# Second mixture of experts on one core: w2 is split one expert ahead, in pieces on ScalarE and GpSimd

## What is computed

```python
logits = flat_x @ Wg + bg
top_vals, top_idx = jax.lax.top_k(logits, TOPK)          # TOPK = 2 of E = 4
probs = jax.nn.softmax(sparse, axis=-1)                  # over the two chosen
for i in range(E):
    score = jnp.where(assigned, probs[:, i], -jnp.inf)
    sel_p, sel_idx = jax.lax.top_k(score, capacity)      # capacity = 256 tokens
    p = jnp.where(jnp.isfinite(sel_p), sel_p, 0.0)[:, None]
    tok = flat_x[sel_idx]
    h = jax.nn.gelu(tok @ W1[i], approximate=False)      # 256 -> 1024
    y = h @ W2[i] * p                                    # 1024 -> 256
    out = out.at[sel_idx].add(y)
```

## Time and profile before

| | us |
|---|---|
| median of 3 runs | 693.44 (691.79 to 694.69) |
| the profiled execution | 689.28 |
| its span, from the first to the last instruction | 687.5 |
| mean granted clock of TensorE | 0.902 |
| busy in the span: PE 589.1, DVE 518.8, ACT 358.8, POOL 183.3 | |

### The profile page before, as it was taken

The page is one execution under the profiler, slowest core; times in us unless marked ns, Lnnn a source line. Parts: engine busy times, 40 slices in busy tenths (PEclk is TensorE's granted clock), DMA queues, the critical chain, the costliest instruction groups (busy, mean ns, idle before and its releaser), DMA issues. The chain is left out here.

```text
span 687.5 us, 12671 instructions
## 1 busy us (share of the span) xinstructions
PE 589.1 (86%) x4686; PEld 403.4 (59%) x4686; DVE 518.8 (75%) x1029; ACT 358.8 (52%) x691; POOL 183.3 (27%) x296
## 2 busy tenths in 40 slices
PE   3989999996589999958989999999999857987793
PEld 2745555554467888856744444444444624976782
DVE  4788888875658766674678999999994587877636
ACT  3226777773344334342214878888888261443452
POOL 4334555562023222130500111111010000234550
PEclk9959999999589999986975999999999955998998
DMA  4534554621231211001520434424421431044331
GB/s 163 67 88 68 86 86 84 92 65 46 54 115 46 61 50 49 0 1 61 65 29 2 65 48 65 61 49 69 58 64 39 135 120 68 1 147 146 92 77 61
DMA packets 27541, 47.15 MB, mean 69 GB/s; under 512 B 13232, under 2 KB 18464, under 8 KB 26208
## 3 DMA queue, kind: packets, MB, share of 16 engines
q1 hardware_dynamic: 22112, 39.11, 27.5%
q0 software_dynamic: 4288, 7.20, 3.9%
q10 hardware_dynamic: 1088, 0.13, 0.1%
HBM read 25.22 MB, written 7.83 MB: 48 GB/s over the span
## 5 line engine op out<-in xcount | busy, mean ns | idle before, releaser
L467 ACT ACTIVATE probs<-ps 128x512 f32<-128x512 f32 x448 | 213.3, 561 | 79.2 <-PE ps L384 78.8
L360 PE MATMUL ps<-k_stack,q_stack 62*128 62x512 f32 x448 | 174.5, 466 | 7.5 <-DVE row_max L563 3.3
L384 PE MATMUL ps<-q_stack,k_stack 64*128 64x512 f32 x448 | 160.1, 435 | 9.8 <-ACT probs L467 5.9
L563 DVE TENSOR_REDUCE row_max<-ps 128x1 f32<-128x1024 f32 x128 | 149.8, 1214 | 16.2 <-PE ps L360 16.2
L384 PEld LDWEIGHTS ps<-q_stack,k_stack 64*128 64x128 f32 x448 | 76.1, 190 | 81.9 <-ACT probs L467 65.2
L399 PE MATMUL ps<-probs,v_ones 128*32 128x256 f32 (+7 forms) x2048 | 116.4, 344 | 1.9 <-ACT probs L467 1.0
L360 PEld LDWEIGHTS ps<-k_stack,q_stack 62*128 62x128 f32 x448 | 80.0, 200 | 37.6 <-DVE row_max L563 16.5
L560 DVE CUSTOM_DVE_ANT_0 y_sums<-ps,wide_mask 128x1024 f32<-128x1024 f32 (+7 forms) x128 | 91.4, 755 | 13.1 <-PE ps L360 11.8
L399 PEld LDWEIGHTS ps<-probs,v_ones 128*32 128x32 f32 x2048 | 51.5, 110 | 44.5 <-issue 14.0
L518 POOL TENSOR_SCALAR_AFFINE_SELECT probs<-probs 128x128 f32<-128x128 f32 x128 | 39.3, 313 | 46.4 <-ACT probs L467 45.1
L899 POOL TENSOR_TENSOR w_chunk_l_m<-y_sums,w_chunk_h_m 128x512 fp32r<-128x512 f32 (+1 forms) x24 | 24.3, 1039 | 101.5 <-ACT w_chunk_h_m L957 94.3
(11 more groups left out here) (208 smaller groups left out, 1125.1 us busy)
## 6 DMA issues: line engine op xcount, KB each, us to landing
y_sums<-in_w_experts SPq DMA_DIRECT2D x8, 1024.0 KB, 5.2
y_sums<-in_w_chunks SPq DMA_DIRECT2D x12, 384.0 KB, 3.1
q_stack<-part_rows SPq DMA_DIRECT2D x32, 128.0 KB, 3.4
k_stack<-part_rows SPq DMA_DIRECT2D x32, 128.0 KB, 3.9
head_sums<-sums POOLq DMA_DIRECT2D x28, 128.0 KB, 2.0
q_stack<-part_rows SPq DMA_DIRECT2D x32, 64.0 KB, 4.0
k_stack<-part_rows SPq DMA_DIRECT2D x32, 64.0 KB, 3.9
q_stack<-max_rows SPq DMA_DIRECT2D x128, 2.0 KB
```

The source lines that it names most:

```text
L360: mm = pe.matmul(scores_bank(s, a, b), stack("q_stack", h, slice(0, TOP))[:, qt * P:(qt + 1) * P], stack("k_stack", h, slice(0, TOP))[:, a ...
L384: pe.matmul(bank(at % 3, 0, b - a), stack("k_stack", h, slice(0, SIDE))[:, kt * P:(kt + 1) * P], stack("q_stack", h, slice(0, SIDE))[:, a: ...
L467: act.activation(probs[:, t % 4, a:b], bank(at % 3, 0, b - a), ACT.Exp).then_inc(exp_done, 1)
L563: dve.tensor_reduce(row_max[:, h % 2, qt:qt + 1], scores_bank(s, 0, end), AX.X, ALU.max).then_inc(scores_free, 1)
```

## The change

Four edits, all in `mixture_1`:

- **w2 one expert ahead.** ACT makes w2's high part of expert e + 1 in four pieces (`split_piece`), one behind each quarter's GELU copy of expert e; the single instruction behind `split_slots` is gone. POOL makes the low quarter of expert e + 1 behind `g_l` of the same quarter of expert e (expert 0's behind `row_ready`, before the experts begin).
- **POOL's order.** `fetch(e + 1)` stands one quarter earlier in POOL's queue, and `add_rows(e - 1)` ahead of expert e's quarters, as before.
- **SP's order.** For experts 2 and 3, w2 is loaded in front of w1.
- **Unread products.** Seven go in front of TensorE's wait for the probabilities, three between `row(0)` and `ranks(0)`, and those in `ranks(0)` go from 14 to 7, with none behind the last three tiles.

```diff
--- before.py
+++ after.py
@@ -1139,7 +1139,7 @@
             sp.dma_start(dram["x_rows"].rearrange("(t p) d -> p t d", p=P), x[:, :, :]).then_inc(rows_out, 16)
             sp.dma_start(dram["x_sum"].rearrange("(t p) d -> p t d", p=P), x[:, :, :]).then_inc(sum_out, 16)
             for e in range(1, E1):
-                for n, done in ((0, w1_in), (1, w2_in)):
+                for n, done in ((0, w1_in), (1, w2_in))[::1 if e == 1 else -1]:
 
                     sp.wait_ge(w_low[n], NQ * e if n else e)
                     sp.dma_start(raw[:, n, :], dram["w_experts1"][e, n]).then_inc(done, 16)
@@ -1163,9 +1163,11 @@
             def weights_low(e, q):
 
                 cols = slice(q * HALF, (q + 1) * HALF)
-                if q == 0:
-                    pool.wait_ge(w_high[1], e + 1)
-                pool.wait_ge(gl_ready, NQ * e + q + 1)
+                pool.wait_ge(w_high[1], NQ * e + q + 1)
+                if e == 0:
+                    pool.wait_ge(row_ready, 1)
+                else:
+                    pool.wait_ge(gl_ready, NQ * (e - 1) + q + 1)
                 pool.tensor_tensor(w_l[:, W_AT(e, 1), cols], raw[:, 1, cols], w_h[:, W_AT(e, 1), cols].bitcast(F32), ALU.subtract
                                    ).then_inc(w_low[1], 1)
 
@@ -1190,21 +1192,31 @@
                                             scaled[:, e, s, :], None, compute_op=ALU.add,
                                             bounds_check=T - 1, oob_is_err=True).then_inc(spread, 16)
 
+            for q in range(NQ):
+                weights_low(0, q)
             for e in range(E1):
-                for q in range(NQ):
-                    weights_low(e, q)
-                    if e < LAST and q == (1 if e else 2):
-                        fetch(e + 1)
+                if e:
+                    add_rows(e - 1)
                 if e < LAST:
-                    add_rows(e)
+                    for q in range(NQ):
+                        if q == (1 if e else 2):
+                            fetch(e + 1)
+                        weights_low(e + 1, q)
 
         @block.scalar
         def _(act):
             def split_weights(e, n):
                 act.wait_ge((w1_in, w2_in)[n], 16 * (e + 1))
-                if n and e >= 2:
-                    act.wait_ge(down_ready, e - 1)
-                act.activation(w_h[:, W_AT(e, n), :], raw[:, n, :], ACT.Copy).then_inc(w_high[n], 1)
+                act.activation(w_h[:, W_AT(e, n), :], raw[:, n, :], ACT.Copy).then_inc(w_high[n], NQ if n else 1)
+
+            def split_piece(e, q):
+
+                cols = slice(q * HALF, (q + 1) * HALF)
+                if q == 0:
+                    act.wait_ge(w2_in, 16 * (e + 1))
+                    if e >= 2:
+                        act.wait_ge(down_ready, e - 1)
+                act.activation(w_h[:, W_AT(e, 1), cols], raw[:, 1, cols], ACT.Copy).then_inc(w_high[1], 1)
 
             def split_slots(e):
 
@@ -1234,6 +1246,8 @@
                     if e:
                         act.wait_ge(down_ready, e)
                     act.activation(g_h[:, q * HALF:(q + 1) * HALF], gelu[:, q % 2, :], ACT.Copy).then_inc(gh_ready, 1)
+                    if e < LAST:
+                        split_piece(e + 1, q)
                     if e == LAST:
                         act.wait_ge(hot_turned, q + 1)
                         act.activation(one_hot_t[:, 0, q // 2, q % 2 * HALF:(q % 2 + 1) * HALF], bank(HOT), ACT.Copy).then_inc(hot_t_out, 1)
@@ -1241,7 +1255,6 @@
 
                     split_weights(e + 1, 0)
                     split_slots(e + 1)
-                    split_weights(e + 1, 1)
                     act.wait_ge(down_ready, e + 1)
                     act.wait_ge(p_ready, e + 1)
                     for s in range(ST):
@@ -1283,7 +1296,7 @@
                         mm = pe.matmul(bank(SMALL, t, 1), before(a)[:, (t - a) * P:(t - a + 1) * P], ones[:, 0:1],
                                        start=(a == 0 and t == 0), stop=a == t, skip_group_check=True)
                     if e == 0:
-                        keep_warm((3, 2, 2, 2, 1, 1, 1, 2)[a])
+                        keep_warm((2, 2, 1, 1, 1, 0, 0, 0)[a])
                     if a == NT - 1:
                         mm.then_inc(rank_ready, 1)
                 if e + 1 < E1:
@@ -1329,6 +1342,7 @@
                         mm = pe.transpose(bank(XG, k * CAP + s * P, P), x_slots[:, s, k * P:(k + 1) * P], consts[:, C_ID:C_ID + P])
                 mm.then_inc(gathered, 1)
 
+            keep_warm(7)
             pe.wait_ge(parts_ready, 2)
             pe.wait_ge(preset, 4)
             for n in range(2):
@@ -1336,6 +1350,7 @@
                     mm = pe.matmul(bank(XG + n, t % 4 * P, P)[0:2 * E1, :], slot_cols[:, t, 0:2, :].rearrange("p l e -> p (l e)"), ident[:, :], start=True, stop=True)
                 mm.then_inc(turned_ready, 1)
             row(0)
+            keep_warm(3)
             ranks(0)
             gather_first()
             slots(0)
```

## The result

The changed kernel's median is 673.12 us (four executions, 670.28 to 676.05) beside 692.62 of the kernel before: a ratio of 0.9721, 95% interval 0.9691 to 0.9751. Its twelve executions have a median of 676.2. So the gain is 14 to 19.5 us, and the forecast of 675.9 (17.5 us less) lies within it.

A forecast was written before the change was run, and what follows sets the result against it. It took waits for POOL's low w2, the late w2 transfer and the clock falling behind such waits as the bound; 3.2 + 1.9 + 5.2 + 3.3 + 3.9 = 17.5 us off 693.44 gave 675.9, range 669.5 to 684.

The forecast's parts named there:

- D: Rival: slower, TensorE's clock stays at 1.2 GHz from the gather to the last "down"; 697 us, chance 0.03.
- E: Rival: no net effect, another wait of the same length overtakes the pieces; chance 0.02.
- C: Rival: w2 lands 3.5 us late in experts 1 and 2 and ACT waits; 682.9 us, chance 0.08.
- A: Rival: POOL holds DVE at every turn, two more quarters in experts 1 and 2; 681.9 us, chance 0.20.
- B: Rival: clock granted early in the gather, never falls between experts, DVE not blocked; 670.6 us, chance 0.13.
- Part 1: Unread products before the gather: gather 3.8 us earlier, partly offset if the clock rises late; -3.2 us.
- Part 2: Expert 0: TensorE stops waiting for POOL, next waits for tokens; w1's low part held by two POOL quarters; -1.9 us.
- Part 5: Expert 3: POOL has only `add_rows`, "down" runs bare; 13.8 us against 17.7, -3.9 us.
- part 3: Expert 1: no w2 wait worth counting, POOL's work covered; 17.4 us against 22.6, -5.2, about 2 of it clock.
- part 4: Expert 2: ACT paces it, the last `g_l` waits for POOL until 11.4; 16.2 us against 19.5, -3.3 us.
- held case: Expert 1: POOL holds the last `g_l`, so TensorE gets to the next "up" at 17.5 us instead of 15.5.
- Rule and row: `g_l` wait: profile rows show two POOL quarters; the rule, read as at most 1.27 us, made the sum 1.5 larger.

The follow-up runs named there:

- e4: The changed kernel with SP's old order, w1 loaded in front of w2 for every expert; 682.92 us, ratio 0.9876.
- e8: The changed kernel without any of its seventeen unread products; 678.06 us, ratio 0.9805.
- e11: The kernel of e5 without any unread product; 669.16 us, ratio 0.9674.
- e2: The changed kernel with the old unread products (14 in `ranks(0)`, none in front), so the weights part alone; ratio 0.9803.
- e5: The changed kernel with POOL making two w2 quarters, then the token gather, and the last two quarters only after the expert's last `g_l`; 671.88 us, ratio 0.9693.
- e7: The changed kernel with the token gather one quarter later in POOL's queue, as before the change; 672.94 us in its one execution.
- e10: The kernel of e5 run again beside the changed kernel on one chip; 670.34 us, ratio 0.9709.
- e6: The changed kernel with the token gather left in place and the three POOL quarters behind it waiting for the expert's last `g_l`; 671.79 us, ratio 0.9702.
- e3: The kernel before with only the new placing of unread products; ratio 0.996.

## Why the prediction was right, and where it was not

**Right in kind and, for the median, in size.** The weights' pieces took TensorE's wait for POOL away, w2's transfer went out of sight (ACT waits for none), and nothing on ACT took its place. Of the rivals, D (the clock never comes back) and E (another wait of the same length) did not happen, C did not but is one line away (e4). A did not either: two `g_l` took over 2 us, and they are the two that the sum already had (a third, in expert 2, took 1.64). B had the clock stay up, and it did not. Two of the signs of being right were missed: the clock in experts 1 and 2 (0.91 for over 0.95) and the gather's start, 1.6 us behind the last comparison for 1.3. How much of the weights' part is ACT's pieces and how much POOL's place was not run apart.

**Part 1, -3.2:** measured -3.0 (29.5 to 26.5 from the router's first product to "up"). Both terms were right: 4.0 us earlier gather (3.8 expected), and 1.1 given back by the late rise (of at most 1.4). What I had wrong is what the products are for. Those behind the tiles had only delayed the ranks; the ones in front bring the gather no sooner (e8, e11: front 18.5 with none). In these profiles the part's whole gain is the seven that it takes out of `ranks(0)`. And the part's price behind the first "up" was missing from the sum: the clock fell in experts 1 and 2 with it and not in e2's profile without it, so that by the profiles it gained this kernel nothing in all (96.6 and 96.3).

**Part 2, -1.9:** measured 19.2 us against 19.0 expected. Its picture holds: w1's low part is held by two quarters (4.46), and the turns wait for the tokens (1.3 against 1.6). Only `fetch` began no earlier, 11.5 us into the expert as before (11.4), where I had 0.4 less.

**Part 5, -3.9:** 13.7 to 13.9 in every profile with the weights ahead; 13.8 expected.

**Parts 3 and 4 are the steps that failed, by 1.7 and 1.9 us.** In part 3 I had "15.5 if the last `g_l` is made at 10.2 and 17.5 if POOL holds it" and took 17.4, the held case, and rightly. What I left out was the clock: it fell behind the idle that I had priced, as it had behind such a wait before the change, and part of the 48 products ran at 1.2 GHz. Of the 1.7 us, 1.0 is the clock (19.1 with the fall, 18.0 in e2 with the same wait and without the fall) and 0.7 a held case that I had made too short. In part 4 `g_l` is done at 12.4 where I had 12.0. There e2 takes 15.9 with a wait 0.6 shorter and no fall; by that, an estimate, 1.6 of the 1.9 are the clock and 0.3 the longer hold. Together 3.6 of the 4.3 us by which the profiled pair fell short of the sum (13.2 for 17.5). It is the low clock of the old kernel that I had counted as gone ("of which about 2 are the clock") while keeping waits of 2.5 to 2.7 us in the sum. The profiles of e2 and e8, with the block and without the fall, show what the steps would have been: 18.0 and 15.9. Why it fell in one and not in the other stays open. e5, without either: 15.5 and 15.5.

That the median nevertheless came out at the forecast is partly luck. The profiled execution of before lay 3 to 4 us below its median and that of the changed kernel above its own, and the first four executions had two at 670.3; the lowest of the eight later ones is 672.4. Those eight have medians of 677.2 and 677.1, 14.6 and 14.4 us below the kernel before, which is nearer to the 13.2 of the profiled pair than to 17.5.

**Rule and row:** I went by the row (a wait through two quarters) and not by the reading of the Trainium skill's rule (SBUF — State Buffer, section "SBUF: two separate sides") that gave 1.5 us less; 3.20, 3.17 and 3.20 us in the three profiles bear the row out.

## What to carry to other kernels

When work of an engine moves off the path, look for what it will stand in front of in its new place: here the next bound was not POOL's time (1.27 us a quarter) but two of its instructions queued back to back where DVE's short one had to pass. Gate such work behind the last short instruction that matters; one changed constant in a wait and one in an order gave another 4 to 7 us (6.8 side by side). And an idle time that you leave in the sum can have the clock behind it: price it twice, once as a wait and once as the products that may follow at half speed.

## What was not expected of the hardware

- A VectorE subtraction that has begun by the profile while GpSimd's gather still runs is passed by the subtractions queued behind the gather: 0.69, 2.11 and 3.20 us with none, one and two of them. The gather itself costs it nothing (0.69 us at 633.56 in e5, wholly within one).
- The unread products in front ran at 2.4 GHz in the changed kernel (seven in 1.90 us), the clock being up from 565 to 572, and it was down again before the ranks, with seven unread products and the ranks to do; the gather that followed still began at 1.2 GHz. This rise is not the code's alone. Up to the gather the changed kernel and e4 to e7 and e10 are the same: in five profiles (the changed kernel's three, e4 and e7) the clock, in windows of 0.25 us, is up from 3.5 to 3.8 us behind the router's first product until 10.2 to 10.5, and the gather's stage takes 8.1 to 8.2; in three (e5, e6, e10) it is up from 8.5 to 9.0 until 12.0 to 12.2, and the stage takes 7.3 to 7.4.
- After nearly the same idle of TensorE (2.7 us) the clock fell in all three profiles of the changed kernel and in neither of e2 and e8, which differ from it only in unread products 40 to 50 us earlier. Behind 3.2 us of idle in expert 0 it fell in e3 and not in the kernel before, which differ in the same way. In both pairs it is the kernel with products in front that lost its clock; each of e2, e8, e3 and before has one profile, so that this may be chance. What decides was not tried.
